# First attention of a graph network: the weights of the last 4 of 25 destination blocks on GpSimd

## The chip, the cores and the metric

The kernel runs on one core of a Trainium2 chip, as one launch. The metric is the device time of the launch in microseconds (us). The engines are named as the profile names them: PE is TensorE, DVE VectorE, ACT ScalarE, POOL GpSimd, SP SyncE (whose queue, SPq, starts DMA transfers).

## The reference

The input is x, 3125 nodes by 256 features, and 100000 edges (src, dst), sorted by dst. Two layers follow each other; each adds a graph attention and a mixer to x, and then a feed-forward part. The change lies in the graph attention of the first layer (4 heads of 64 features):

```python
h = (x @ W).reshape(N, 4, 64)
e = leaky_relu(al_s[src] + al_d[dst], 0.2)      # per edge and head
ee = exp(e - segment_max(e, dst)[dst])
alpha = ee / (segment_sum(ee, dst)[dst] + 1e-16)
out = segment_sum(h[src] * alpha[:, :, None], dst)
out = relu(out.reshape(N, 256) + bias)
```

The weight of an edge depends on the pair (src, dst) alone. So the sum over edges can be written as a sum over all pairs of nodes: the weight of the pair times the number of edges between them.

## The kernel before

Nodes are split into T = 25 blocks of R = 125. An earlier stage writes the matrix of counts (3125 by 3125, bf16) to DRAM. `stage_gat_sums` (from line 1616) does one attention; the program calls it four times, as g0a (first layer, 4 heads of 64), g1a, g2a (4 heads of 128) and g3a. With a head's width F below 128, J is 2: two heads are handled in one step. Only g0a has J = 2; the others have J = 1.

A **unit** n is one source block sb and one head: a matrix x of 125 sources by 3125 destinations. A **step** is J units with the same sb. In g0a there are NU = 100 units and NS = 50 steps: 25 steps for heads 0 and 1, then 25 for heads 2 and 3. The work on a unit goes over three engines, each with its own program, tied by semaphores:

- ACT, `rise` (line 1815): x = relu(grow * steep + minus), one instruction of 3125 columns; it counts `risen` up. It waits on `multiplied` (line 1819), since x is a ring of XR = 5 buffers.
- DVE, `weigh` (line 1748): x = (x + flat) * counts, one `scalar_tensor_tensor` at line 1755 that reads x in f32 and the counts in bf16, both in SBUF; it counts `weighed` up. The first two units are cut in three pieces of 1125, 1000 and 1000 columns.
- PE (line 1917): waits for the `weighed` of both units of the step and multiplies each destination block (in parts of 64 and 61 columns) by the features of the source block and a column of ones, into 8 PSUM banks. That is 25 x 2 x 2 = 100 products of f32, which show as 200 records each of MATMUL and LDWEIGHTS. The end of a step counts `multiplied` up, which gives two buffers back.

SP (line 1693) loads the counts of one source block per step into a ring of CR = 4 buffers and waits on `weighed` before it fills one again (line 1701). After the 25 steps of a pair of heads, ACT moves the sums out of PSUM (`move`, lines 1837 and 1840), and DVE divides them by the sum of weights (`divide`, lines 1762, 1771, 1779): eight groups of tiles for two heads, one group behind each of eight units. POOL only sets one small tile in this stage (line 1710).

The order of each engine is the order of its code: DVE's loop is at line 1796, ACT's at 1861, PE's at 1917 and, for the last two steps, 1930.

Of the kernel before, what the change touches and what calls it, by code (L numbers as in the profile page):

```python
# [5 lines left out]
ALU = mybir.AluOpType  # L6
# [7 lines left out]
N = 3125  # L14
R = 125
T = N // R
# [1599 lines left out]
def stage_gat_sums(nc, m, g, AL, HX, OUT, X=None, spare=None, ct_out=()):  # L1616

    S, G, F = g.heads, HX.shape[2], HX.shape[3] - 1
    J = 1 if F == P else 2
    NS, NU, GR, XR, CR, YR = G // J * T, G * T, G // J, 2 * J + 1, 3 if spare is None else 4, 4 if g.out == "elu" else 2  # L1620
# [4 lines left out]
    with Stage(nc, g.name + "a") as s:  # L1625
        s.sems.extend(ct_out)
        grow, x = s.sb("grow", [R, S, N]), s.sb("x", [R, XR, N])
        if spare is None:
            ct = s.sb("ct", [R, CR, N], BF16)[:]
# [16 lines left out]
        rows_in = [s.sem(f"rows_in{h}") for h in range(S)]  # L1646
        stepped, crossed, far_ready, factors = [s.sem(n) for n in ("stepped", "crossed", "far_ready", "factors")]
        spread, row_act, row_dve = [s.sem(n) for n in ("spread", "row_act", "row_dve")]
        ct_in = [s.sem(f"ct_in{k}") for k in range(CR)]
        risen, weighed, multiplied, summed, moved, divided = [s.sem(n) for n in ("risen", "weighed", "multiplied", "summed", "moved", "divided")]  # L1650
        low_ready, low_exp, y_ready = [s.sem(n) for n in ("low_ready", "low_exp", "y_ready")]
        y_out = [s.sem(f"y_out{k}") for k in range(YR)]
        block = s.block()

        def place(n):

            return n // (J * T), n // J % T, n % J

        def head(gr, j):
            return gr * J + j if S > 1 else 0  # L1660
# [18 lines left out]
        def upto(n, k=0):  # L1679

            return sum(len(sections(i)) for i in range(n)) + k + 1
# [10 lines left out]
        @block.sync  # L1692
        def _(sp):
            await_counts(sp, ct_out)
            for m_ in range(NS):
                if m_ == CR and S > 1:
                    sp.wait_ge(rows_ready, 1)
                    sp.dma_start(m.RW, turned[:]).then_inc(rows_kept, 16)
                    sp.wait_ge(rows_kept, 16)
                if m_ >= CR:  # L1700
                    sp.wait_ge(weighed, upto((m_ - CR + 1) * J) - 1)
                h, j = (m_ // T + 1) * J + (m_ % T - CR) // 5, (m_ % T - CR) % 5
                if CR <= m_ % T < CR + 5 * J and h < S:
                    sp.dma_start(grow[25 * j:25 * (j + 1), h, :], m.RW[h * T:(h + 1) * T].rearrange("t r -> (t r)").partition_broadcast(25)).then_inc(rows_in[h], 16)
                sb = m_ % T
                tile_dma(sp, ct[:, m_ % CR, :], m.CT[sb * R:(sb + 1) * R], ct_in[m_ % CR])

        @block.gpsimd
        def _(pool):
            nc.gpsimd.memset(under[:], UNDER).then_inc(stepped, 1)  # L1710
            if g.out == "elu":
                for n in range(G * CH):
                    gr, c = n // CH, n % CH
                    t0, t1 = tiles[c][0], tiles[c][-1] + 1
                    pool.wait_ge(y_ready, n + 1)
                    tile_dma(pool, OUT[t0 * R:t1 * R, gr * F:(gr + 1) * F].rearrange("(t p) f -> p t f", p=R), y[:, n % YR, 0:t1 - t0, :], y_out[n % YR])
                for k in range(YR):
                    pool.wait_ge(y_out[k], 32 * (G * CH // YR))

        @block.vector  # L1720
        def _(dve):
# [26 lines left out]
            def weigh(n):  # L1748
                gr, sb, j = place(n)
                h, step = head(gr, j), n // J  # L1750
                dve.wait_ge(ct_in[step % CR], 32 * (step // CR + 1))
                for k, (a, b) in enumerate(sections(n)):
                    dve.wait_ge(risen, upto(n, k))
                    part = x[:, n % XR, a * R:b * R]
                    nc.vector.scalar_tensor_tensor(out=part, in0=part, scalar=flat[:, h, sb:sb + 1], in1=ct[:, step % CR, a * R:b * R],  # L1755
                                                   op0=ALU.add, op1=ALU.mult).then_inc(weighed, 1)
# [118 lines left out]
        def _(pe):  # L1875
# [41 lines left out]
            for step in range(2 // J, NS - 2):  # L1917
                gr, sb = step // T, step % T
                pe.wait_ge(weighed, upto(step * J + J - 1))
                for c in range(CH):  # L1920
                    if sb == 0 and gr > 0:
                        pe.wait_ge(moved, (gr - 1) * CH + c + 1)
                    for i, piece in enumerate(pieces(c)):
                        for j in range(J):
                            done = product(step, i, j, c, *piece)
                    if c == CH - 1:
                        done.then_inc(multiplied, 1)
                    elif sb == T - 1:
                        done.then_inc(summed, 1)
            for c in range(CH):  # L1930
                for step in (NS - 2, NS - 1):
                    if c == 0:
                        pe.wait_ge(weighed, upto(step * J + J - 1))
                    for i, piece in enumerate(pieces(c)):
                        for j in range(J):
                            done = product(step, i, j, c, *piece)
                if c == CH - 1:
                    done.then_inc(multiplied, 2)
                else:
                    done.then_inc(summed, 1)  # L1940
# [1254 lines left out]
```

## Time and profile before

| | us |
|---|---|
| median of 3 runs | 3723.67 (3722.82 to 3724.9) |
| profiled execution, its own time | 3723.46 |
| its span | 3722.0 |
| mean granted clock of TensorE | 0.928 of full speed |
| first attention, first weight instruction (546.6) to the end of ACT's last move (949.4) | 402.8 |

The span runs from the first to the last instruction in the trace; the time of the execution is 1.46 us longer. "Busy" is the time in which an engine had an instruction running. "Idle before" is the time in which an engine stood still ahead of a group of instructions, with the instruction elsewhere that ended it. Durations of neighbouring instructions on DVE and ACT overlap by some tens of ns, so the distance from start to start is a little shorter than the duration. In the trace HX stands for a large tile that several stages share: in g0a both the features and the ring of counts lie in it.

### The profile page before, as it was taken

What the parts mean: (1) busy time and instruction counts of PE and PEld (TensorE: products, weight loads), DVE (VectorE), ACT (ScalarE), POOL (GpSimd) and SP (SyncE); (2) the same over time, 40 slices, a digit from 0 to 9 for tenths busy, and PEclk for the clock granted to TensorE, in tenths of its full rate; (3) what the DMA queues carried; (4) which work ended last, traced back from release to release, by engine and by line L of the source; (5) the groups of instructions that cost most, each with busy time, mean ns of one, the idle gap of its engine ahead of it and who ended that gap; (6) DMA issues with size and microseconds to landing.
All of it is one profiled execution on the core that took longest, in us unless ns stands there. A gap on an engine that the chain in (4) does not pass through costs nothing. (4 is left out here: it accounts for less than half of the span.)

```text
span 3722.0 us, 75746 instructions
## 1 busy us (share of the span) xinstructions
PE 3261.3 (88%) x32397; PEld 2992.8 (80%) x32397; DVE 2070.4 (56%) x2243; ACT 1707.3 (46%) x2005; POOL 232.3 (6%) x320
## 2 busy tenths in 40 slices
PE   3788877878469999687999999699999997999899
PEld 3568877878469998356899999679999996999676
DVE  6665558989542221653566767326767762666411
ACT  0534457878233333230555555225655552555332
POOL 1000000000012222002000100100001001000000
PEclk9879989999579999798999999899999998999889
DMA  3223345433246554301655655325656544544020
GB/s 113 51 45 51 52 85 130 119 89 88 80 169 210 185 185 144 71 12 43 160 152 155 174 140 151 85 69 159 165 143 175 146 126 129 159 136 127 6 59 27
DMA packets 176755, 424.91 MB, mean 114 GB/s; under 512 B 72469, under 2 KB 104990, under 8 KB 175052
## 3 DMA queue, kind: packets, MB, share of 16 engines
q1 hardware_dynamic: 159134, 383.68, 38.2%
q0 software_dynamic: 13904, 33.84, 3.0%
q8 instruction: 248, 4.06, 0.5%
q10 hardware_dynamic: 3399, 2.76, 0.3%
q14 instruction: 70, 0.57, 0.1%
HBM read 366.69 MB, written 53.50 MB: 113 GB/s over the span
## 5 line engine op out<-in xcount | busy, mean ns | idle before, releaser
L1904 PE MATMUL g2a_ps<-HX,g2a_x 125*125 125x129 f32 (+2 forms) x5200 | 575.2, 273 | 3.4 <-ACT g2a_grow L1858 3.3
L1904 PE MATMUL g1a_ps<-HX,g1a_x 125*125 125x129 f32 (+2 forms) x5200 | 574.9, 273 | 3.4 <-ACT g1a_grow L1858 3.4
L1904 PEld LDWEIGHTS g2a_ps<-HX,g2a_x 125*125 125x125 f32 x5200 | 574.8, 189 | 3.7 <-ACT g2a_grow L1858 3.5
L1904 PEld LDWEIGHTS g1a_ps<-HX,g1a_x 125*125 125x125 f32 x5200 | 574.6, 188 | 3.8 <-ACT g1a_grow L1858 3.6
L1755 DVE SCALAR_TENSOR_TENSOR g2a_x<-g2a_x,g2a_flat,g2a_ct 125x3125 f32<-125x3125 f32 (+2 forms) x104 | 348.2, 3350 | 183.0 <-ACT g2a_x L1812 171.4
L1755 DVE SCALAR_TENSOR_TENSOR g1a_x<-g1a_x,g1a_flat,g1a_ct 125x3125 f32<-125x3125 f32 (+2 forms) x104 | 348.2, 3350 | 182.7 <-ACT g1a_x L1812 174.3
L1812 ACT ACTIVATE g2a_x<-g2a_grow,g2a_near,g2a_steep 125x3125 f32<-125x3125 f32 (+2 forms) x104 | 300.9, 2897 | 243.1 <-PE g2a_ps L1904 242.8
L1812 ACT ACTIVATE g1a_x<-g1a_grow,g1a_near,g1a_steep 125x3125 f32<-125x3125 f32 (+2 forms) x104 | 300.9, 2897 | 242.9 <-PE g1a_ps L1904 242.6
L1904 PE MATMUL g0a_ps<-HX,g0a_x 125*64 125x65 f32 (+1 forms) x10000 | 318.1, 228 | 84.7 <-DVE g0a_x L1755 44.4
L1904 PEld LDWEIGHTS g0a_ps<-HX,g0a_x 125*64 125x64 f32 (+1 forms) x10000 | 309.8, 142 | 93.1 <-issue 45.6
L1755 DVE SCALAR_TENSOR_TENSOR g0a_x<-g0a_x,g0a_flat,HX 125x3125 f32<-125x3125 f32 (+2 forms) x104 | 341.4, 3346 | 31.4 <-ACT g0a_x L1812 31.2
L1812 ACT ACTIVATE g0a_x<-g0a_grow,g0a_near,g0a_steep 125x3125 f32<-125x3125 f32 (+2 forms) x104 | 294.9, 2892 | 83.0 <-PE g0a_ps L1904 80.3
L1904 PE MATMUL g3a_ps<-HX,g3a_x 125*125 125x129 f32 (+2 forms) x2600 | 289.2, 274 | 3.4 <-ACT g3a_grow L1858 3.4
L1904 PEld LDWEIGHTS g3a_ps<-HX,g3a_x 125*125 125x125 f32 x2600 | 288.8, 189 | 3.8 <-ACT g3a_grow L1858 3.5
L2628 ACT ACTIVATE moe_hT<-moe_psh,moe_sm 128x128 f32<-128x128 f32 x448 | 154.6, 368 | 244.6 <-PE moe_psh L2546 229.7
L1755 DVE SCALAR_TENSOR_TENSOR g3a_x<-g3a_x,g3a_flat,HX 125x3125 f32<-125x3125 f32 (+2 forms) x54 | 174.4, 3234 | 106.3 <-ACT g3a_x L1812 106.3
L2546 PE MATMUL moe_psh<-moe_xe,moe_wa 128*128 128x128 f32 x1792 | 211.8, 277 | 0.0
L1812 ACT ACTIVATE g3a_x<-g3a_grow,g3a_near,g3a_steep 125x3125 f32<-125x3125 f32 (+2 forms) x54 | 151.0, 2803 | 123.5 <-PE g3a_ps L1904 123.2
L2546 PEld LDWEIGHTS moe_psh<-moe_xe,moe_wa 128*128 128x128 f32 x1792 | 207.2, 194 | 0.1
L2608 DVE TENSOR_SCALAR moe_ys<-moe_psy,WGT 128x256 f32<-128x256 f32 x56 | 27.1, 484 | 319.8 <-PE moe_psy L2557 319.8
L706 ACT ACTIVATE HX<-merge_ps 125x500 bf16<-125x500 f32 (+1 forms) x175 | 93.9, 568 | 194.8 <-PE merge_ps L561 192.6
L2557 PE MATMUL moe_psy<-HX,moe_hT 128*128 x672 | 154.3, 379 | 0.0
(579 smaller groups left out, 3920.5 us busy)
## 6 DMA issues: line engine op xcount, KB each, us to landing
HX<-counted SPq DMA_DIRECT2D x100, 683.6 KB
g1a_ct<-counted SPq DMA_DIRECT2D x100, 683.6 KB
g2a_ct<-counted SPq DMA_DIRECT2D x100, 683.6 KB
moe_wa<-in_L_ffn_W SPq DMA_DIRECT2D x56, 1024.0 KB
counted<-HX SPq DMA_DIRECT2D x12, 1367.2 KB
HX<-counted SPq DMA_DIRECT2D x100, 79.3 KB
g1a_ct<-counted SPq DMA_DIRECT2D x100, 79.3 KB
g2a_ct<-counted SPq DMA_DIRECT2D x100, 79.3 KB
```

What stands on the lines that cost most here:

```text
L706: nc.scalar.activation(ct[:, two % 2, :, d0:d0 + n], ps[0:R, job % BANKS, 0:n * T].rearrange("p (d s) -> p s d", s=T), ACT.Copy).then_inc( ...
L1755: nc.vector.scalar_tensor_tensor(out=part, in0=part, scalar=flat[:, h, sb:sb + 1], in1=ct[:, step % CR, a * R:b * R], op0=ALU.add, op1=ALU ...
L1812: nc.scalar.activation(x[:, n % XR, a * R:b * R], grow[:, h, a * R:b * R], ACT.Relu, bias=minus[:, h, sb:sb + 1], scale=steep[:, h, sb:sb ...
L1904: return nc.tensor.matmul(ps[64 * j:64 * j + b - a, c, col:col + f1 - f0], x[:, (step * J + j) % XR, t * R + a:t * R + b], HX[:, sb, gr * ...
L2546: last = nc.tensor.matmul(psh[:, o % 4, 0:ET], wa[:, j % 3, c, o * P:(o + 1) * P], xe[:, j % XE, c, :], start=(c == 0), stop=(c == 1))
L2557: last = nc.tensor.matmul(psy[:, j % 2, 0:D], hT[:, j % 2, c, :], right, start=(c == 0), stop=(c == MH - 1))
L2608: nc.vector.tensor_scalar(ys[:, j % 2, :], psy[:, j % 2, 0:D], WGT[:, j:j + 1], None, ALU.mult).then_inc(y_ready, 1)
L2628: nc.scalar.activation(hT[:, j % 2, o, :], psh[:, o % 4, 0:ET], ACT.Gelu, bias=sm[:, j % IN, 4 + o:5 + o]).then_inc(h_ready, 1)
```

## The change

In a stage with J = 2, `share` is 21 x 125 = 2625. From unit 2 on DVE's instruction ends at column 2625. POOL gets a loop over units 2 to 99: it waits for the counts and for `risen`, adds the factor to columns 2625 to 3124 (`tensor_scalar`), drains, multiplies them by the counts (`tensor_tensor`) and counts the new semaphore `weighed_too` up. PE waits on it too before a step from step 1 on, and SP before it fills a count buffer again. Where J = 1 nothing changes.

```diff
--- before.py
+++ after.py
@@ -1646,11 +1646,13 @@
         rows_in = [s.sem(f"rows_in{h}") for h in range(S)]
         stepped, crossed, far_ready, factors = [s.sem(n) for n in ("stepped", "crossed", "far_ready", "factors")]
         spread, row_act, row_dve = [s.sem(n) for n in ("spread", "row_act", "row_dve")]
-        ct_in = [s.sem(f"ct_in{k}") for k in range(CR)]
+        ct_in, weighed_too = [s.sem(f"ct_in{k}") for k in range(CR)], s.sem("weighed_too")
         risen, weighed, multiplied, summed, moved, divided = [s.sem(n) for n in ("risen", "weighed", "multiplied", "summed", "moved", "divided")]
         low_ready, low_exp, y_ready = [s.sem(n) for n in ("low_ready", "low_exp", "y_ready")]
         y_out = [s.sem(f"y_out{k}") for k in range(YR)]
         block = s.block()
+
+        share = (T - 4) * R if J == 2 else N
 
         def place(n):
 
@@ -1699,6 +1701,8 @@
                     sp.wait_ge(rows_kept, 16)
                 if m_ >= CR:
                     sp.wait_ge(weighed, upto((m_ - CR + 1) * J) - 1)
+                    if J == 2 and m_ > CR:
+                        sp.wait_ge(weighed_too, (m_ - CR) * J)
                 h, j = (m_ // T + 1) * J + (m_ % T - CR) // 5, (m_ % T - CR) % 5
                 if CR <= m_ % T < CR + 5 * J and h < S:
                     sp.dma_start(grow[25 * j:25 * (j + 1), h, :], m.RW[h * T:(h + 1) * T].rearrange("t r -> (t r)").partition_broadcast(25)).then_inc(rows_in[h], 16)
@@ -1708,6 +1712,16 @@
         @block.gpsimd
         def _(pool):
             nc.gpsimd.memset(under[:], UNDER).then_inc(stepped, 1)
+            if J == 2:
+                for n in range(2, NU):
+                    gr, sb, j = place(n)
+                    h, step = head(gr, j), n // J
+                    pool.wait_ge(ct_in[step % CR], 32 * (step // CR + 1))
+                    pool.wait_ge(risen, upto(n))
+                    part = x[:, n % XR, share:N]
+                    nc.gpsimd.tensor_scalar(part, part, flat[:, h, sb:sb + 1], None, ALU.add)
+                    nc.gpsimd.drain()
+                    nc.gpsimd.tensor_tensor(part, part, ct[:, step % CR, share:N], ALU.mult).then_inc(weighed_too, 1)
             if g.out == "elu":
                 for n in range(G * CH):
                     gr, c = n // CH, n % CH
@@ -1751,6 +1765,8 @@
                 dve.wait_ge(ct_in[step % CR], 32 * (step // CR + 1))
                 for k, (a, b) in enumerate(sections(n)):
                     dve.wait_ge(risen, upto(n, k))
+                    if n > 1 and J == 2:
+                        b = share // R
                     part = x[:, n % XR, a * R:b * R]
                     nc.vector.scalar_tensor_tensor(out=part, in0=part, scalar=flat[:, h, sb:sb + 1], in1=ct[:, step % CR, a * R:b * R],
                                                    op0=ALU.add, op1=ALU.mult).then_inc(weighed, 1)
@@ -1917,6 +1933,8 @@
             for step in range(2 // J, NS - 2):
                 gr, sb = step // T, step % T
                 pe.wait_ge(weighed, upto(step * J + J - 1))
+                if J == 2:
+                    pe.wait_ge(weighed_too, step * J)
                 for c in range(CH):
                     if sb == 0 and gr > 0:
                         pe.wait_ge(moved, (gr - 1) * CH + c + 1)
@@ -1931,6 +1949,8 @@
                 for step in (NS - 2, NS - 1):
                     if c == 0:
                         pe.wait_ge(weighed, upto(step * J + J - 1))
+                        if J == 2:
+                            pe.wait_ge(weighed_too, step * J)
                     for i, piece in enumerate(pieces(c)):
                         for j in range(J):
                             done = product(step, i, j, c, *piece)
```

DVE's instructions at the start of g0a's loop, before (flat is the factor of each source, grow the factor row of each destination):

```order
L1794 COPY g0a_grow<-g0a_ps 125x1000 x2
L1755 SCALAR_TENSOR_TENSOR g0a_x<-g0a_x,g0a_flat,HX 125x1125
L1755 SCALAR_TENSOR_TENSOR g0a_x<-g0a_x,g0a_flat,HX 125x1000 x2
L1755 SCALAR_TENSOR_TENSOR g0a_x<-g0a_x,g0a_flat,HX 125x1125
L1755 SCALAR_TENSOR_TENSOR g0a_x<-g0a_x,g0a_flat,HX 125x1000 x2
L1755 SCALAR_TENSOR_TENSOR g0a_x<-g0a_x,g0a_flat,HX 125x3125 x51
L1762 RECIPROCAL g0a_rec<-g0a_raw 125x3
L1771 TENSOR_TENSOR g0a_raw<-g0a_raw,g0a_rec 125x3x64
L1779 SCALAR_TENSOR_TENSOR X<-g0a_raw,X 125x3x64
```

and with the change:

```order
L1810 COPY g0a_grow<-g0a_ps 125x1000 x2
L1771 SCALAR_TENSOR_TENSOR g0a_x<-g0a_x,g0a_flat,HX 125x1125
L1771 SCALAR_TENSOR_TENSOR g0a_x<-g0a_x,g0a_flat,HX 125x1000 x2
L1771 SCALAR_TENSOR_TENSOR g0a_x<-g0a_x,g0a_flat,HX 125x1125
L1771 SCALAR_TENSOR_TENSOR g0a_x<-g0a_x,g0a_flat,HX 125x1000 x2
L1771 SCALAR_TENSOR_TENSOR g0a_x<-g0a_x,g0a_flat,HX 125x2625 x51
L1778 RECIPROCAL g0a_rec<-g0a_raw 125x3
L1787 TENSOR_TENSOR g0a_raw<-g0a_raw,g0a_rec 125x3x64
L1795 SCALAR_TENSOR_TENSOR X<-g0a_raw,X 125x3x64
```

The number and the order are the same; from the third unit on the instructions have 2625 columns instead of 3125, and the divisions behind them are as they were.

POOL's instructions around the same place, before (moe_qT and moe_xin belong to the expert stage that follows):

```order
L1708 UNCONDITIONAL_BRANCH
L1710 MEMSET g0a_under 125x1
L61 UNCONDITIONAL_BRANCH
L63 ISA x7
L2503 UNCONDITIONAL_BRANCH
L2102 MEMSET moe_qT 9x1500
L2508 DMA moe_xin<-normal_rows,TOKEN 128x256 x6
```

and with the change:

```order
L1712 UNCONDITIONAL_BRANCH
L1714 MEMSET g0a_under 125x1
L1722 ISA
L1722 TENSOR_SCALAR g0a_x<-g0a_x,g0a_flat 125x500
L1724 TENSOR_TENSOR g0a_x<-g0a_x,HX 125x500
```

There are 98 such pairs of 500 columns, one for each unit from the third on, all ahead of the expert stage's first instruction on POOL.

## Rows read from the trace of the kernel before

**Rows 1.** The page: span, busy time of each engine.

```profile
span 3722.0 us, 75746 instructions
PE 3261.3 (88%) x32397; PEld 2992.8 (80%) x32397; DVE 2070.4 (56%) x2243; ACT 1707.3 (46%) x2005; POOL 232.3 (6%) x320
```

**Rows 2.** Windows: the first attention, busy us and instructions of each engine.

```profile
core 0: us, PE busy (x) PEld busy (x) DVE busy (x) ACT busy (x) POOL busy (x), PEclk, DMA share, GB/s
546.60:949.40 402.80, 318.12 (x10000) 309.76 (x10000) 362.83 (x186) 313.44 (x173) 0.00 (x0) 0.94 0.38 103
```

**Rows 3.** Groups by shape, 546 to 950 us: busy us, mean ns, idle before.

```profile
L1755 DVE SCALAR_TENSOR_TENSOR g0a_x<-g0a_x,g0a_flat,HX 125x3125 f32<-125x3125 f32 x98 | 334.2, 3471 | 31.4 <-ACT g0a_x L1812 31.2
L1755 DVE SCALAR_TENSOR_TENSOR g0a_x<-g0a_x,g0a_flat,HX 125x1000 f32<-125x1000 f32 x4 | 4.9, 1257 | 0.0
L1812 ACT ACTIVATE g0a_x<-g0a_grow,g0a_near,g0a_steep 125x3125 f32<-125x3125 f32 x98 | 287.7, 2992 | 80.5 <-PE g0a_ps L1904 80.3
```

**Rows 4.** Waits, 545 to 950 us (SPq from 530): total us, times, longest.

```profile
ACT g0a_x L1812 <- PE g0a_ps L1904: 80.3, 36, 6.0
PE g0a_ps L1904 <- DVE g0a_x L1755: 44.4, 26, 6.6
DVE g0a_x L1755 <- ACT g0a_x L1812: 31.2, 17, 7.8
DVE g0a_rec L1762 <- ACT g0a_raw L1840: 4.5, 2, 3.8
SPq L69 <- DVE g0a_x L1755: 250.6, 36, 15.8
```

**Rows 5.** Timeline (start us, us, instruction), then windows (columns as rows 2).

```profile
647.56 68.04 DVE L1755 SCALAR_TENSOR_TENSOR g0a_x<-g0a_x,g0a_flat,HX 125x3125 f32<-125x3125 f32 x20 [0.75 <-ACT g0a_x L1812]
...
754.44 3.47 DVE L1755 SCALAR_TENSOR_TENSOR g0a_x<-g0a_x,g0a_flat,HX 125x3125 f32<-125x3125 f32 x1 [7.82 <-ACT g0a_x L1812]
...
791.79 23.77 DVE L1755 SCALAR_TENSOR_TENSOR g0a_x<-g0a_x,g0a_flat,HX 125x3125 f32<-125x3125 f32 x7
...
650.53 5.89 ACT L1812 ACTIVATE g0a_x<-g0a_grow,g0a_near,g0a_steep 125x3125 f32<-125x3125 f32 x2 [0.17 <-PE g0a_ps L1904]
...
757.00:791.00 34.00, 24.55 (x626) 24.14 (x628) 31.98 (x48) 21.98 (x9) 0.00 (x0) 0.80 0.27 73
648.00:716.00 68.00, 59.96 (x1994) 58.26 (x1990) 67.50 (x20) 58.05 (x20) 0.00 (x0) 1.00 0.42 118
```

**Rows 6.** POOL's groups over the whole program: busy us, mean ns, idle before.

```profile
L1106 POOL COPY lo_xs<-XT 128x250 f32 x25 | 9.7, 397 | 209.8 <-PEq L1112 198.5 <-PE lo_ps L1123 11.3
L2102 POOL MEMSET moe_qT<- 9x1500 f32 x1 | 1.3, 1338 | 532.0 <-POOLq L64 532.0
L432 POOL MEMSET merge_qT<- 33x1000 f32 x1 | 0.9, 925 | 15.1 <-POOLq L64 15.1
L2888 POOL MEMSET ffn_e<- 128x512 f32 x1 | 0.5, 525 | 394.2 <-POOLq L64 394.2
L1710 POOL MEMSET g0a_under<- 125x1 f32 x1 | 0.1, 93 | 347.8 <-POOLq L64 347.8
```

**Rows 7.** Timeline: POOL beside DVE in the expert stage and at 1682 us.

```profile
L2508 POOL DMA_INDIRECT moe_xin<-normal_rows,TOKEN x56: 945/973/1123, 1064.6 to 1442.2; - x56
...
1180.26 1.28 DVE L2594 TENSOR_TENSOR moe_yb<-moe_yb 128x512 f32<-128x512 f32 x2
1181.27 1.12 POOL L2508 DMA_INDIRECT moe_xin<-normal_rows,TOKEN  x1 [0.30 <-issue]
...
1188.52 0.97 POOL L2508 DMA_INDIRECT moe_xin<-normal_rows,TOKEN  x1 [0.31 <-issue]
...
1681.99 0.42 DVE L2814 TENSOR_TENSOR X<-X,lo_ps 125x256 f32 x1 [18.10 <-PE lo_ps L1123]
1682.01 0.40 POOL L1106 COPY lo_xs<-XT 128x250 f32 x1 [0.42 <-PE lo_ps L1123]
```

**Rows 8.** POOL's DMA instructions of the second attention: ns min/median/max.

```profile
L69 POOL DMA_DIRECT2D attended<-g1a_y x32: 708/714/793, 1943.7 to 2366.9; - x32
L70 POOL DMA_DIRECT2D attended<-g1a_y x32: 569/577/634, 1944.5 to 2367.6; - x32
```

## The prediction

> **What bounds the kernel now.** The page's table of engines comes first: TensorE is busy for 88% of the span and POOL for 6% [rows 1], so POOL has time to give away, but an average over the whole program says nothing about one stage. The groups of instructions by line then place the edit: its new branch is taken where J is 2, and that is the first attention (g0a) alone, whose 104 weight instructions on DVE stand in [rows 3]. The stretch of that stage (first weight instruction to ACT's last move) is 402.8 us of the 3722.0, with DVE busy 362.8, TensorE 318.1, ACT 313.4 and POOL 0 [rows 2]. So this stage has another limit than the program: DVE. Its idle time is 31.2 us in front of the weights, waiting for ACT's relu, and 4.5 in front of the divisions [rows 4]. Who waits for whom confirms it: TensorE waits 44.4 us for DVE's weights, ACT 80.3 us for TensorE to give a buffer back, and the DMA queue spends 250.6 us waiting to be allowed the next count rows, so the loads are never late [rows 4].
>
> The timeline gives the beat. In the best stretches DVE runs without a gap: 20 weights in 68.04 us, 3.40 a unit, 6.80 a step of two units (2 heads) [rows 5]. ACT makes a pair of units in 5.89 and TensorE a step in 6.0 (1994 matmul records in 59.96 us, 200 to a step) [rows 5]. Around the middle each unit also carries two divisions: seven units from 754.44 to 791.79, 5.3 us each [rows 5]. The rest of the 402.8 is the start, the turn between the two passes over the blocks, and the end.
>
> **The change part by part.**
> DVE's part: 98 instructions shrink from 3125 to 2625 columns; the first two units keep their pieces. From 1000 to 3125 columns the duration goes from 1257 to 3471 ns, 1.042 ns a column [rows 3], so each saves 0.52 us and the beat falls to 2.88 us: 98 x 0.52 = **51 us of DVE time removed**.
>
> POOL's part: 98 pairs, an add with a per-partition number over 500 columns and, behind a drain, a product of 500 f32 by 500 bf16. No row of before shows either operation. The nearest row for a pass is the copy of 250 f32 columns, 397 ns; memsets of 512 and 1000 columns took 525 and 925 ns, or 0.82 ns a column [rows 6]. Low end of one pass: the memset's 0.53. High end: twice the copy, 0.79. I take the copy plus 250 more columns at 0.82, 0.60. The second pass reads two tensors: low end the same 0.53, high end two such passes one behind the other at 0.79, 1.59; I take twice 0.60, **1.2**, because the copy's row already takes more per column than the memset's, so that reading seems to cost. Pair: **1.8** (1.06 to 2.4). The Trainium skill (GPSIMD Engine Reference, Reconciling with measured numbers) gives 4497 ns for a tensor_tensor of 2048 f32 on GpSimd; an estimate from it is 1.1 us for 500 columns, and the sum below would be some 10 us less.
>
> The term that decides: can POOL's passes run beside DVE's weights? DVE's instruction reads two tensors from SBUF (x and the counts). The trace has a small case of each kind. POOL's copy beside a DVE instruction with one input in SBUF and one in PSUM: 0.40 and 0.42 us, both as when alone [rows 7]. POOL's row gather, which reads its list of rows from SBUF, takes 0.97, but 1.11 to 1.12 in 6 of 56 cases; those are the six that begin while DVE multiplies two tensors of SBUF (a pair of 512 columns, ending some 0.27 us after the gather's start) and no others [rows 7]. So what POOL wants to read seems to be kept back until DVE's two-input instruction is over. Low end: no exclusion, POOL costs nothing; high end: every pass stands between two DVE instructions and never beside one. I take the high end, since the gather is the row that is alike in what matters (two SBUF inputs on DVE). The Trainium skill (SBUF — State Buffer, Who interferes with whom) says that a VectorE instruction with two SBUF inputs and a GpSimd instruction that reads SBUF exclude each other, the later one waiting in full. By that rule the sum is the one below; with the exclusion struck out it would be the first rival's.
>
> Then the two engines are one resource. Each unit needs 2.88 + 1.8 = 4.68 us of it, a step 9.4, where ACT needs 5.9 and TensorE 6.0: both are covered. Even at the clock of 0.80 that the middle stretch shows at its 10.6 us a step TensorE is not the limit [rows 5]. Sum over the stage: -51 from DVE, +98 x 1.8 = +176 from POOL, and POOL can use about 20 of the 31.2 us in which DVE now waits for ACT: **+105 us**. The order in which they alternate changes little: whichever goes first, TensorE waits for both before it starts a step, and the ring of five buffers ties DVE to TensorE.
>
> Costs set at nothing: POOL's queue holds nothing else in this stage (one memset of 0.09 us; its next instruction, in the expert stage, comes 532.0 us after it) [rows 6]. The DMA queue's added wait stands in front of reloading a count buffer: four buffers, so it is early by about three steps, and no DVE row waits for a load [rows 4]; at risk only if a step's POOL part ran more than three steps behind, which TensorE's wait forbids. TensorE's added wait holds the whole step, though the four blocks are its last; behind it are all 100 products and, through the buffers, ACT.
>
> The profiled execution took 3723.46 us around its span of 3722.0, and the median is 3723.67: 3723.5 + 105 = 3828.5, **3829 us**.
>
> **Rivals.**
> *Side by side (faster).* The passes run beside DVE, 1.8 under 2.88. Then the beat is the ring's: ACT 2.99 + DVE 2.95 + TensorE 6.0 and a few tenths of handing over, 12.2 us for two steps, 6.1 instead of 6.80. About 34 of the 50 steps are paced by DVE now (17 waits for ACT [rows 4] mark the others): 34 x 0.7 = -24, and -8 to -34 as TensorE's clock goes. 3700. For it: the copy of [rows 7], and POOL's DMA instructions beside the same weight instructions in g1a, at a steady 714 and 577 ns, far from the 3.4 us that a wait for each would give [rows 8]; but those read no tensor from SBUF. Against it: the gather. It decides as long as POOL's pair stays under about 3.3 us.
>
> *Partial exclusion.* Only a part of each pass is kept apart (its reading, not its dispatch and writing), or the two share and both slow down: a third to two thirds of the 176 remain, 59 to 118. With the 51 taken off, and the 20 of idle time or not, that is -12 to +67; about 3755.
>
> *POOL too slow by itself.* Side by side, but the pair takes over 3.4 us. Each tenth over costs 98 x 0.1 = 10 us. My upper end, 2.4, is not enough for that, so this needs a pass twice as long as any bound here; it shares the chance of the case above, and its size.
>
> **How the numbers follow.** Full exclusion 0.63 (3756 at a pair of 1.06, from 104 - 51 - 20 = +33; 3887 at 2.4, from 235 - 51 - 20 = +164), partial exclusion or slow POOL 0.16, side by side 0.21. The predicted time is the first case's, and its own range is 3756 to 3887. The range for 8 in 10 has to take in the faster case, down to a gain of 25: 3698 to 3887. About 0.2% or 7 us is what a measurement of this kernel can tell from no change. Faster 0.20 (side by side, nearly whole), same 0.05 (the lower part of partial exclusion), slower 0.75.
>
> **What would show it.** After: DVE's weights at 2.95 us where undisturbed, and the stage at about 508 us instead of 402.8. Exclusion: weights or POOL passes that last longer than their size explains, or that begin when the other's end, never beside; TensorE waiting for POOL's product; ACT's wait for TensorE grown; the step at 9.4. Side by side: POOL's pair of 1.8 within a 2.95 us weight, the step at 6.1. The pass's size is wrong if POOL's adds and products are far from 0.60 and 1.2. I am wrong outright if the stage gets shorter, or if another stage than g0a changes by more than a few us.

## The result and the profile after

| | before | changed |
|---|---|---|
| median of 5 runs, us | 3723.67 | 3844.49 (3840.68 to 3845.61) |
| ratio, 95% interval | | 1.0333 (1.032 to 1.0347) |
| profiled span, us | 3722.0 | 3838.4 |
| first attention, first weight to ACT's last move, us | 402.8 | 520.0 |

The change costs 121 us by the medians. The predicted 3829 is 15 us below, and the time lies inside the range; that the total fits is in part luck, as shown below. In the profiled executions the span grew by 116.4 us and the first attention by 117.2, so all of it is there. The rest of the program did not move, as two windows show, after first and then before (columns as in [rows 2]):

```profile
1067.00:3838.00 2771.00, 2528.68 (x18708) 2325.99 (x18708) 1376.53 (x1557) 1177.28 (x1271) 217.91 (x299) 0.94 0.44 126
```

```profile
949.40:3722.00 2772.60, 2527.01 (x18708) 2325.47 (x18708) 1377.76 (x1560) 1178.23 (x1272) 217.49 (x299) 0.94 0.44 126
```

The changed kernel's page, its first two lines, beside [rows 1]:

```profile
span 3838.4 us, 76233 instructions
PE 3312.2 (86%) x32397; PEld 3043.2 (79%) x32397; DVE 2070.4 (54%) x2243; ACT 1706.3 (44%) x2005; POOL 705.8 (18%) x516
```

POOL went from 232.3 to 705.8 us. The window over the first attention answers to [rows 2]:

```profile
core 0: us, PE busy (x) PEld busy (x) DVE busy (x) ACT busy (x) POOL busy (x), PEclk, DMA share, GB/s
546.00:1067.00 521.00, 367.53 (x10000) 359.81 (x10000) 364.72 (x188) 313.65 (x173) 473.11 (x196) 0.83 0.29 79
```

DVE is as busy as before (364.7 us; 362.8 before), although its instructions lost 51 us of columns. ACT is unchanged. TensorE does the same 10000 records in 367.5 instead of 318.1 us, its granted clock down from 0.94 to 0.83. POOL is busy for 473 us with work that I had put at 176. The groups of the stage (busy us, mean ns, idle before):

```profile
L1722 POOL TENSOR_SCALAR g0a_x<-g0a_x,g0a_flat 125x500 f32<-125x500 f32 x98 | 280.2, 2859 | 33.7 <-ACT g0a_x L1828 33.7
L1724 POOL TENSOR_TENSOR g0a_x<-g0a_x,HX 125x500 f32<-125x500 f32 x98 | 194.9, 1988 | 14.4 <-issue 0.2
L1771 DVE SCALAR_TENSOR_TENSOR g0a_x<-g0a_x,g0a_flat,HX 125x2625 f32<-125x2625 f32 x98 | 328.4, 3387 | 144.4 <-ACT g0a_x L1828 144.1 <-issue 0.3
```

DVE's mean of 3387 ns is 0.43 us over the 2.95 that its 2625 columns take alone. POOL's means, 2.86 and 1.99 us, are together 2.24 us over the length of its two passes alone, which the next rows show.

The instructions that write the weights (ns min/median/max, first and last start):

```profile
L1771 DVE SCALAR_TENSOR_TENSOR g0a_x<-g0a_x,g0a_flat,HX x104: 1251/3366/3893, 546.0 to 1045.1; 125x2625 f32<-125x2625 f32 x98, 125x1000 f32<-125x1000 f32 x4, 125x1125 f32<-125x1125 f32 x2
L1722 POOL TENSOR_SCALAR g0a_x<-g0a_x,g0a_flat x98: 1528/2385/4813, 552.8 to 1049.0; 125x500 f32<-125x500 f32 x98
L1724 POOL TENSOR_TENSOR g0a_x<-g0a_x,HX x98: 1065/1228/3795, 557.7 to 1050.6; 125x500 f32<-125x500 f32 x98
```

The minima are the operations by themselves: 1.53 us for POOL's add, 1.07 for its product. A pass that is issued while DVE's instruction runs lasts until some time after that instruction's end. In the trace 48 of the 98 adds and 48 of the 98 products are held up like this; nearly all the others take their minimum. Seven lines of the timeline show how they stand to each other (start us, us, instruction; x2 is two instructions back to back):

```profile
703.22 5.88 ACT L1828 ACTIVATE g0a_x<-g0a_grow,g0a_near,g0a_steep 125x3125 f32<-125x3125 f32 x2 [5.85 <-PE g0a_ps L1920]
706.32 6.50 DVE L1771 SCALAR_TENSOR_TENSOR g0a_x<-g0a_x,g0a_flat,HX 125x2625 f32<-125x2625 f32 x2 [4.89 <-ACT g0a_x L1828]
706.75 4.17 POOL L1722 TENSOR_SCALAR g0a_x<-g0a_x,g0a_flat 125x500 f32<-125x500 f32 x1
711.07 2.67 POOL L1724 TENSOR_TENSOR g0a_x<-g0a_x,HX 125x500 f32<-125x500 f32 x1
713.72 1.54 POOL L1722 TENSOR_SCALAR g0a_x<-g0a_x,g0a_flat 125x500 f32<-125x500 f32 x1
713.88 2.42 PE L1920 MATMUL g0a_ps<-HX,g0a_x 125*64 125x65 f32 x42 [2.87 <-POOL g0a_x L1724]
...
721.49 5.88 ACT L1828 ACTIVATE g0a_x<-g0a_grow,g0a_near,g0a_steep 125x3125 f32<-125x3125 f32 x2 [4.55 <-PE g0a_ps L1920]
```

ACT hands over the first unit at 706.2. DVE starts on it at 706.32, and POOL's add is issued at 706.75, but it ends only at 710.92, 1.39 us behind the end of DVE's first instruction at 709.53. (That one took 3.21 us and met the end of an earlier product of POOL's; the second took 3.37.) DVE has the second unit under way by then. POOL's product, issued at 711.07, has to wait for that one too and ends at 713.74, 0.92 behind it. TensorE starts at 713.88. This first unit is the one that completes TensorE's step. From ACT's handing over to TensorE's start it takes **7.7 us**, where DVE's one instruction of 3.47 stood before. Who waits for whom, beside [rows 4]:

```profile
ACT g0a_x L1828 <- PE g0a_ps L1920: 195.9, 46, 9.2
DVE g0a_x L1771 <- ACT g0a_x L1828: 144.1, 41, 8.0
PE g0a_ps L1920 <- POOL g0a_x L1724: 120.9, 44, 7.8
PE g0a_ps L1920 <- DVE g0a_x L1771: 18.6, 5, 6.6
```

TensorE now waits 120.9 us for POOL; it waited 44.4 for DVE. ACT waits 195.9 us (80.3) for buffers from TensorE, DVE 144.1 us (31.2) for ACT. Three of the four engines wait for each other. POOL does not: from its first pass at 552.8 to the end of its last at 1051.7 us it waits 11.4 us for ACT (33.7 less the 22.3 before its first pass) and loses 14.4 in the gaps between add and product. It has become the engine that the stage goes by, at 499 us for 98 units or **5.1 us a unit**: 2.6 us of passes, 2.2 of being held up behind DVE, and the gaps.

### The profile page after: what moved, and what is told of

Its sections match the earlier page's. It is cut to its first block and busy times, and to the rows that moved or that the text cites. A ratio compares the mean times of both kernels' runs of the same rounds, so it can differ in the third digit from the quotient of the medians.

```text
span 3838.4 us, 76233 instructions
## 1 busy us (share of the span) xinstructions
PE 3312.2 (86%) x32397; PEld 3043.2 (79%) x32397; DVE 2070.4 (54%) x2243; ACT 1706.3 (44%) x2005; POOL 705.8 (18%) x516
## 5 line engine op out<-in xcount | busy, mean ns | idle before, releaser
L1920 PE MATMUL g0a_ps<-HX,g0a_x 125*61 125x65 f32 (+1 forms) x10000 | 367.5, 245 | 152.2 <-POOL g0a_x L1724 120.9
L1920 PEld LDWEIGHTS g0a_ps<-HX,g0a_x 125*61 125x61 f32 (+1 forms) x10000 | 359.8, 159 | 160.0 <-issue 147.2
L1771 DVE SCALAR_TENSOR_TENSOR g2a_x<-g2a_x,g2a_flat,g2a_ct 125x3125 f32<-125x3125 f32 (+2 forms) x104 | 348.2, 3350 | 183.2 <-ACT g2a_x L1828 180.1
L1771 DVE SCALAR_TENSOR_TENSOR g0a_x<-g0a_x,g0a_flat,HX 125x2625 f32<-125x2625 f32 (+2 forms) x104 | 335.7, 3266 | 144.4 <-ACT g0a_x L1828 144.1
L1828 ACT ACTIVATE g0a_x<-g0a_grow,g0a_near,g0a_steep 125x3125 f32<-125x3125 f32 (+2 forms) x104 | 295.2, 2887 | 198.4 <-PE g0a_ps L1920 195.9
L1722 POOL TENSOR_SCALAR g0a_x<-g0a_x,g0a_flat 125x500 f32<-125x500 f32 x98 | 280.2, 2859 | 33.7 <-ACT g0a_x L1828 33.7
L1724 POOL TENSOR_TENSOR g0a_x<-g0a_x,HX 125x500 f32<-125x500 f32 x98 | 194.9, 1988 | 14.4 <-issue 0.2
```

The lines of the kernel that those rows point to most:

```text
L1722: nc.gpsimd.tensor_scalar(part, part, flat[:, h, sb:sb + 1], None, ALU.add)
L1724: nc.gpsimd.tensor_tensor(part, part, ct[:, step % CR, share:N], ALU.mult).then_inc(weighed_too, 1)
L1828: nc.scalar.activation(x[:, n % XR, a * R:b * R], grow[:, h, a * R:b * R], ACT.Relu, bias=minus[:, h, sb:sb + 1], scale=steep[:, h, sb:sb ...
L1920: return nc.tensor.matmul(ps[64 * j:64 * j + b - a, c, col:col + f1 - f0], x[:, (step * J + j) % XR, t * R + a:t * R + b], HX[:, sb, gr * ...
```

## Experiments

In what follows "products end" is the last product's start in the profiled execution, and the stage is measured as in the table above. Ratios are to the kernel before, timed on the same chip beside each run: 3720.04 us beside e1 to e4, 3715.82 beside e5 to e8. The stage in a profiled execution varies by more than that: unchanged it took 402.8 us before and 395.7 in e8, on another chip. So a gain of a few us is read from the medians. The cuts are against the changed kernel and show only the lines that matter. In e1, e2, e3, e4 and e6 ACT's bias is changed as e1's cut shows.

### e1: nobody makes the last four blocks' weights

POOL's whole loop goes, and SP's wait on it.

```diff
-                    nc.gpsimd.tensor_scalar(part, part, flat[:, h, sb:sb + 1], None, ALU.add)
-                    nc.gpsimd.drain()
-                    nc.gpsimd.tensor_tensor(part, part, ct[:, step % CR, share:N], ALU.mult).then_inc(weighed_too, 1)
...
-                    pe.wait_ge(weighed_too, step * J)
...
-                nc.scalar.activation(x[:, n % XR, a * R:b * R], grow[:, h, a * R:b * R], ACT.Relu, bias=minus[:, h, sb:sb + 1],
+                nc.scalar.activation(x[:, n % XR, a * R:b * R], grow[:, h, a * R:b * R], ACT.Relu, bias=(flat if J == 2 and n > 1 else minus)[:, h, sb:sb + 1],
```

> Left out: the weights of the last four blocks are not made by any engine (ACT's bias is the positive factor, so that no sum is zero), and nobody waits for GpSimd. It shows what VectorE's shorter instruction is worth alone. Every theory expects the same here: VectorE 2.95 us an instruction, the first attention 375 to 385 us instead of 402.8, the kernel about 25 us under before, 3700. If it is not under before at all, the 51 us taken off VectorE were never on the path, and the whole +121 is GpSimd's.

Measured: 3710.76, ratio 0.9974 (0.9962 to 0.9986), a gain of about 10 us where some 25 were expected; the stage takes 392.8 us, not 375 to 385. So the 51 us taken from DVE are worth about 10, not the 24 of my faster rival. The window that held 20 units before [rows 5]:

```profile
648.00:716.00 68.00, 57.83 (x1842) 56.60 (x1839) 55.12 (x20) 53.27 (x20) 0.00 (x0) 0.95 0.41 111
```

DVE is busy for 55 of 68 us instead of 67.5, and the beat is no faster. (The x20 counts each instruction that touches the window; TensorE's records make 9.2 steps of 200, where they made 10.0 before, at a clock of 0.95 instead of 1.00.) The gain lies later: 39 units from 788.46 to 920.23 us, or 6.76 a step, where the kernel before made 35 from 791.79 to 917.37, or 7.18. The 6.1 us of my faster rival shows in one stretch only, eight units in 24.4 us:

```profile
826.07 11.66 DVE L1759 SCALAR_TENSOR_TENSOR g0a_x<-g0a_x,g0a_flat,HX 125x2625 f32<-125x2625 f32 x4 [0.77 <-ACT g0a_x L1816]
838.32 11.72 DVE L1759 SCALAR_TENSOR_TENSOR g0a_x<-g0a_x,g0a_flat,HX 125x2625 f32<-125x2625 f32 x4 [0.58 <-ACT g0a_x L1816]
850.45 5.84 DVE L1759 SCALAR_TENSOR_TENSOR g0a_x<-g0a_x,g0a_flat,HX 125x2625 f32<-125x2625 f32 x2 [0.41 <-ACT g0a_x L1816]
```

The waits say what took over (the stretch is 545 to 950 us):

```profile
ACT g0a_x L1816 <- PE g0a_ps L1908: 72.4, 36, 6.3
DVE g0a_x L1759 <- ACT g0a_x L1816: 69.4, 34, 9.7
PE g0a_ps L1908 <- issue: 41.9, 27, 3.9
PE g0a_ps L1908 <- DVE g0a_x L1759: 28.4, 16, 6.6
```

TensorE stands still for 41.9 us with nothing that the profile can name, 27 times, for up to 3.9 us; ACT waits for TensorE, and DVE for ACT. The kernel before had these pauses too (its waits, then two lines of its timeline):

```profile
PE g0a_ps L1904 <- issue: 37.0, 23, 3.7
...
655.91 7.68 PE L1904 MATMUL g0a_ps<-HX,g0a_x 125*61 125x65 f32 x256 [0.70 <-issue]
664.19 6.44 PE L1904 MATMUL g0a_ps<-HX,g0a_x 125*61 125x65 f32 x209 [0.60 <-issue]
```

Here 256 products lie between two pauses. Counted through the stage, all 23 pauses of the kernel before stand a whole multiple of 128 MATMUL records apart, and so do the 27 of e1. So they belong to places in TensorE's sequence of instructions and not to DVE's data. With them TensorE cannot keep up 6.0 us a step, and relieving DVE brings little. What they are was not tested.

### e2: GpSimd's passes on data of its own, nobody waits

The waits on POOL are left out as in e1; `apart` has 460 columns and `m.all` is the table of constants.

```diff
-                    part = x[:, n % XR, share:N]
-                    nc.gpsimd.tensor_scalar(part, part, flat[:, h, sb:sb + 1], None, ALU.add)
+                    part = apart[:]
+                    nc.gpsimd.tensor_scalar(part, m.all[0:R, 0:460], flat[:, h, sb:sb + 1], None, ALU.add)
...
-                    nc.gpsimd.tensor_tensor(part, part, ct[:, step % CR, share:N], ALU.mult).then_inc(weighed_too, 1)
+                    nc.gpsimd.tensor_tensor(part, part, m.all[0:R, 500:960], ALU.mult).then_inc(weighed_too, 1)
```

> As the run without GpSimd, but GpSimd makes its 98 pairs of passes on data of its own (460 columns, read from the constants), behind the same signal of ACT, and nobody waits for it. Exclusion (both want the same way to SBUF): VectorE's instructions last 3.5 to 3.9 us wherever a pass stands beside them, its pitch is 2.88 plus one pass's reading, about 3.6 us, and the products end 30 to 60 us later than without GpSimd; GpSimd gets one pass per VectorE instruction, lags to half and runs on alone for some 100 us behind it. Rival (the waits on GpSimd's slow chain are the cost, not the port): VectorE stays at 2.95 us, the products end where they do without GpSimd, and GpSimd's passes stay at 1.54 and 1.07 us.

Measured: 3821.68, ratio 1.0275 (1.0257 to 1.0292), but where the time lies matters. The products end at 947.9, 11.5 us later than in e1 (936.4) and where they did before (947.8); counted from each run's first weight it is 10 us. The timeline:

```profile
698.12 14.16 DVE L1773 SCALAR_TENSOR_TENSOR g0a_x<-g0a_x,g0a_flat,HX 125x2625 f32<-125x2625 f32 x4
699.64 2.84 POOL L1725 TENSOR_TENSOR g0a_apart<-g0a_apart,C 125x460 f32<-125x460 f32 x1
702.73 3.81 POOL L1723 TENSOR_SCALAR g0a_apart<-C,g0a_flat 125x460 f32<-125x460 f32 x1 [0.25 <-issue]
706.68 2.84 POOL L1725 TENSOR_TENSOR g0a_apart<-g0a_apart,C 125x460 f32<-125x460 f32 x1
709.77 3.80 POOL L1723 TENSOR_SCALAR g0a_apart<-C,g0a_flat 125x460 f32<-125x460 f32 x1 [0.25 <-issue]
```

No data tie the two engines together here, and yet each slows the other. DVE's pitch is 3.54 us (14.16 by 4) instead of 2.88. POOL gets one pass per DVE instruction in this stretch: a pair every 7.04 us, two DVE pitches. So it falls behind and runs on alone after the products, with passes that now last 1.43 and 1.15:

```profile
1050.05 1.43 POOL L1723 TENSOR_SCALAR g0a_apart<-C,g0a_flat 125x460 f32<-125x460 f32 x1 [0.25 <-issue]
1051.63 1.15 POOL L1725 TENSOR_TENSOR g0a_apart<-g0a_apart,C 125x460 f32<-125x460 f32 x1
```

The stage's closing barrier waits for that queue, 105 us past the products; that is the 102 us of this run, not a slower ring. The exclusion is shown. My 30 to 60 us for the products was too much: what DVE lost (0.66 a unit in this stretch, 0.53 in the mean) is about what it had gained by its fewer columns.

### e3: all waits, but passes that only write

```diff
-                    nc.gpsimd.tensor_scalar(part, part, flat[:, h, sb:sb + 1], None, ALU.add)
...
-                    nc.gpsimd.tensor_tensor(part, part, ct[:, step % CR, share:N], ALU.mult).then_inc(weighed_too, 1)
+                    for _k in range(4):
+                        nc.gpsimd.memset(apart[:], 1.0)
+                        nc.gpsimd.drain()
+                    nc.gpsimd.memset(apart[:], 1.0).then_inc(weighed_too, 1)
```

> All waits of the change are kept, but GpSimd's pair is replaced by five memsets of 460 columns, together some 2.6 us, the length of an undisturbed pair; they write SBUF and read nothing. Left out: the weights of the last four blocks (ACT's bias is the positive factor). Exclusion of readers: within 10 us of the run without GpSimd, 3700 to 3715, and VectorE at 2.95 us. Rival (the chain of waits is the cost): most of the +116 stays, 3800 or more.

Measured: 3714.6, ratio 0.9987 (0.9977 to 0.9998), 4 us above e1. DVE is undisturbed:

```profile
L1774 DVE SCALAR_TENSOR_TENSOR g0a_x<-g0a_x,g0a_flat,HX x104: 1252/2954/2958, 544.7 to 917.1; 125x2625 f32<-125x2625 f32 x98, 125x1000 f32<-125x1000 f32 x4, 125x1125 f32<-125x1125 f32 x2
```

A chain of 2.9 us on POOL (from the first memset's start to the fifth's end; the real pair, undisturbed in e4, takes 2.8) with every wait of the change costs next to nothing as long as it reads nothing from SBUF. The waits alone are not the cause.

### e4: GpSimd's real passes beside a DVE instruction with one input

```diff
+                    if n > 1 and J == 2:
+                        nc.vector.tensor_reduce(least_of[:, n:n + 1], part, AX_X, ALU.max).then_inc(weighed, 1)
+                        continue
                     nc.vector.scalar_tensor_tensor(out=part, in0=part, scalar=flat[:, h, sb:sb + 1], in1=ct[:, step % CR, a * R:b * R],
                                                    op0=ALU.add, op1=ALU.mult).then_inc(weighed, 1)
```

> The changed kernel with its GpSimd passes and all its waits, but VectorE's instruction on units from the third on is a maximum over the same 2625 columns into a number of its own: one input from SBUF instead of two, about the same length. Left out: the weights of the 21 blocks. If two inputs are what excludes GpSimd: passes at 1.54 and 1.07 us always, the first attention 375 to 390 us, 3695 to 3715. Rival (any VectorE instruction that reads SBUF excludes GpSimd): passes of 2.7 and 4.2 us as in the changed kernel and 3830 or more.

Measured: 3719.36, ratio 0.9997 (0.9984 to 1.0009).

```profile
L1724 POOL TENSOR_SCALAR g0a_x<-g0a_x,g0a_flat x98: 1527/1535/2032, 551.9 to 926.6; 125x500 f32<-125x500 f32 x98
L1774 DVE TENSOR_REDUCE g0a_least_of<-g0a_x x98: 2874/2887/2890, 552.4 to 926.5; 125x1 f32<-125x2625 f32 x98
L1726 POOL TENSOR_TENSOR g0a_x<-g0a_x,HX x98: 1062/1132/1292, 554.1 to 928.3; 125x500 f32<-125x500 f32 x98
```

POOL reads and writes the same data as in the change, and its passes stay at 1.54 and 1.13 us, DVE's at 2.89. Only three adds (1.72 to 2.03 us) and one product (1.29) are longer, and each of the four meets an instruction of DVE that still has two inputs. So it is not DVE's reading as such that keeps POOL out. The maximum differs from the weights in a second thing: it writes one column and not 2625. That DVE's writing does no harm is shown by a smaller case, the copy of [rows 7]: 0.40 us, as when alone, beside a DVE instruction that writes 256 columns and reads one input from SBUF and one from PSUM. With it the second input from SBUF is what remains, though no run took that input away and left the rest of the instruction as it was. The time is 9 us above e1 and 4 over my upper bound; even with no exclusion the change would have given nothing that can be measured.

### e5 and e6: one pass each

e5, the add alone:

```diff
-                    nc.gpsimd.tensor_scalar(part, part, flat[:, h, sb:sb + 1], None, ALU.add)
-                    nc.gpsimd.drain()
-                    nc.gpsimd.tensor_tensor(part, part, ct[:, step % CR, share:N], ALU.mult).then_inc(weighed_too, 1)
+                    nc.gpsimd.tensor_scalar(part, part, flat[:, h, sb:sb + 1], None, ALU.add).then_inc(weighed_too, 1)
```

e6, the product alone:

```diff
-                    nc.gpsimd.tensor_scalar(part, part, flat[:, h, sb:sb + 1], None, ALU.add)
-                    nc.gpsimd.drain()
```

> The change with GpSimd's first pass alone (the add); left out: the product with the counts in the last four blocks. All waits stay. Theory A (two engines share one resource: the cost is the sum of busy time, as the prediction summed it): a pass of 1.54 us by 98 is 151, less 51 and 20: +80, about 3800. Theory B (only a pass's reading excludes VectorE, some 0.67 us of the add, and GpSimd gets one pass per VectorE instruction; what costs is TensorE's wait for GpSimd's last pass of a step): of the pair's chain behind the second VectorE instruction (product 0.9, add 1.6, product 1.07) the add alone stays, so +20 to +60, 3745 to 3780; passes of 4.2 us and of 1.54 in equal numbers.

> The change with GpSimd's second pass alone (the product); left out: the add in the last four blocks (ACT's bias is the positive factor). Theory A (sum of busy time): 1.07 by 98 is 105, less 51 and 20: +34, 3755. Theory B (one pass per VectorE instruction, TensorE waits for the last one): behind the second VectorE instruction of a step only one product of 0.9 to 1.07 us stays, so +0 to +45, 3720 to 3765, and less than the add alone.

Measured: the add alone 3733.27, ratio 1.0047 (1.0031 to 1.0064), +17 us; the product alone 3735.51, ratio 1.0053 (1.0036 to 1.0069), +20 us. First e5, then e6:

```profile
L1769 DVE SCALAR_TENSOR_TENSOR g0a_x<-g0a_x,g0a_flat,HX x104: 1253/3350/3369, 547.6 to 945.0; 125x2625 f32<-125x2625 f32 x98, 125x1000 f32<-125x1000 f32 x4, 125x1125 f32<-125x1125 f32 x2
L1722 POOL TENSOR_SCALAR g0a_x<-g0a_x,g0a_flat x98: 1538/3310/4817, 554.3 to 945.9; 125x500 f32<-125x500 f32 x98
```

```profile
L1769 DVE SCALAR_TENSOR_TENSOR g0a_x<-g0a_x,g0a_flat,HX x104: 1251/3757/3941, 546.1 to 944.4; 125x2625 f32<-125x2625 f32 x98, 125x1000 f32<-125x1000 f32 x4, 125x1125 f32<-125x1125 f32 x2
L1722 POOL TENSOR_TENSOR g0a_x<-g0a_x,HX x98: 1067/2740/3799, 552.8 to 942.6; 125x500 f32<-125x500 f32 x98
```

The sum of busy time gave +80 and +34; e5 refutes it clearly, e6 by 14 us. The add alone is also a little under the +20 to +60 of the other theory, and its passes were not half long and half short: 92 of 98 are held up. A pass keeps DVE out only for part of its length: DVE's median is 3350 ns beside adds (+0.40) and 3757 beside products (+0.80). In e6 DVE hardly waits for ACT (15.0 us in all), so its longer instructions are the cost: 0.26 us over the 3.47 of before, times 98, is 25. That the product would cost less than the add was wrong: they are equal. The stage takes 416.0 and 416.8 us, 20 and 21 above the unchanged one of e8. And 17 and 20 do not add up to 121, nor do 27 and 30, their distance from e1's gain, to 131: two passes a unit cost much more than twice one.

### e7: one block instead of four

```diff
-        share = (T - 4) * R if J == 2 else N
+        share = (T - 1) * R if J == 2 else N
```

> The change with one block of 125 columns for GpSimd instead of four. Theory A (sum of busy time) with passes a quarter as long plus a fixed part, about 0.5 and 0.4 us: 98 x 0.9 = 88, less 98 x 0.13 = 13 and 20: +55, 3775. Theory B (the alternation, not the columns, is what costs): VectorE's instruction is hardly shorter (3.34 us) and GpSimd still waits for one of them ahead of each pass, so passes last 3.8 to 4 us where they wait; the chain behind the second VectorE instruction shrinks from 3.9 to some 1.5 us: +30 to +75. The two are told apart less by the time than by the passes: under B they last over 3 us though they have 125 columns.

Measured: 3794.71, ratio 1.0218 (1.0201 to 1.0235), +79 by the medians: a quarter of the columns, two thirds of the cost. (DVE is also relieved of less here, 13 us instead of 51, but e1 puts the worth of all 51 at 10.) The stage takes 475.2 us, 79.5 over the unchanged one of e8.

```profile
701.28 3.64 POOL L1722 TENSOR_SCALAR g0a_x<-g0a_x,g0a_flat 125x125 f32<-125x125 f32 x1
...
705.06 3.00 POOL L1724 TENSOR_TENSOR g0a_x<-g0a_x,HX 125x125 f32<-125x125 f32 x1
708.04 0.61 POOL L1722 TENSOR_SCALAR g0a_x<-g0a_x,g0a_flat 125x125 f32<-125x125 f32 x1
708.80 0.40 POOL L1724 TENSOR_TENSOR g0a_x<-g0a_x,HX 125x125 f32<-125x125 f32 x1
```

Passes of 125 columns last 0.61 and 0.40 us alone and 3.64 and 3.00 where they wait for DVE. What costs is that two passes a unit are held up behind DVE instructions, far more than what they do. POOL is no longer busy throughout: it waits 60 us for ACT once it has begun (82.0 less 22.3), so here it is the delay of the unit that TensorE waits for that counts. The cost is a little over the upper end that I gave.

### e8: the same split in the last attention instead

```diff
-        share = (T - 4) * R if J == 2 else N
+        shared = g.out == "plain"
+        share = (T - 4) * R if shared else N
```

> The same split of the weights, undone in the first attention and put into the last one (g3a: one head per step of 5.72 us, VectorE idle for 106 us, TensorE the limit; 48 pairs of passes). The exclusion is there too: adds of about 4.2 us that wait for the VectorE instruction of the same unit. But the add and the product then fit behind it: 2.95 + 1.6 + 1.07 = 5.6 under 5.72, and the ring of three buffers gives 11.4 us. Expected: within 5 us of before, 3715 to 3728. Rival (GpSimd's passes cost wherever they are put): 48 of 98 pairs, so about half of +121, 3780.

Measured: 3722.29 against 3715.82, ratio 1.0022 (1.0012 to 1.0032). Two units of g3a:

```profile
3294.18 2.95 DVE L1772 SCALAR_TENSOR_TENSOR g3a_x<-g3a_x,g3a_flat,HX 125x2625 f32<-125x2625 f32 x1 [2.77 <-ACT g3a_x L1829]
3294.25 4.29 POOL L1723 TENSOR_SCALAR g3a_x<-g3a_x,g3a_flat 125x500 f32<-125x500 f32 x1 [0.22 <-ACT g3a_x L1829]
...
3298.68 1.07 POOL L1725 TENSOR_TENSOR g3a_x<-g3a_x,HX 125x500 f32<-125x500 f32 x1
...
3299.90 2.95 DVE L1772 SCALAR_TENSOR_TENSOR g3a_x<-g3a_x,g3a_flat,HX 125x2625 f32<-125x2625 f32 x1 [2.77 <-ACT g3a_x L1829]
```

The exclusion is the same: each add waits for the DVE instruction of its unit and takes 4.29 us. But DVE has one unit per 5.72 us there, so the product comes at once and undisturbed, 5.57 us behind DVE's start (3294.18 to 3299.75), before the next instruction of DVE. TensorE waited for POOL only this long:

```profile
PE g3a_ps L1921 <- POOL g3a_x L1725: 4.0, 2, 2.3
```

TensorE is the limit in this attention, so that a delay has slack to go into as well. Its products take from 3167.1 to 3459.2 us, 292.1, where they took 289.0 before (3173.7 to 3462.7). The median is 6.5 us above; some 3 of them are seen in that stage, where the rest lies is open.

## Why the prediction was right, and what was wrong in it

**What bounds the kernel: half right.** DVE did set the beat at 6.80, but the next limit was put at 6.1 us a step, from TensorE's 6.0. The row with TensorE's unnamed pauses (37.0 us) was left out of the argument. With them e1 comes to 6.76 us a step in its better half, against 7.18 before, and gains 10 us, not 24. The faster rival was worth 0.3%, close to nothing.

**DVE's part, -51 us: right in size.** 2950 ns an instruction were forecast and 2953 measured in e1. It was not worth that much on the path. Nor did POOL use 20 us of DVE's idle time: DVE's wait for ACT grew from 31.2 to 144.1 us.

**POOL's part: mis-sized, one up, one down.** The add was put at 0.60 (bounds 0.53 to 0.79) and takes 1.54; the product at 1.2 and takes 1.07. The copy at 397 ns for 250 columns was the wrong neighbour of an add with a number per partition. e7 gives the add two points, 0.61 us at 125 columns and 1.54 at 500: 2.5 ns a column against the 0.82 that I took from the memsets. The pair is 2.6 us, over the 2.4 of my high end. The estimate of 1.1 us for the product, worked out from the figure of the Trainium skill (GPSIMD Engine Reference, Reconciling with measured numbers), agrees with the 1.07 measured.

**The deciding term, exclusion: right, and shown.** The gather's 0.15 us [rows 7] pointed the right way. e2 shows it with no data tie, e3 removes POOL's reading and e4 DVE's second input (and most of its writing), and it vanishes both times. The rule of the Trainium skill (SBUF — State Buffer, Who interferes with whom) names just this pair, and says that a GpSimd instruction that only writes goes free, and so does a VectorE instruction with one input from SBUF, outside its two-port modes; e3 and e4 agree. It also calls the shared ports an exclusive lock, held for the whole instruction. For POOL behind DVE that holds (passes of 4.17 and 2.67). For DVE behind POOL the runs show less: 0.40 us for an add that lasts 1.54.

**"The two engines are one resource", 4.68 us a unit, +105: the step that failed.** It gave nearly the right total by the wrong sum, and by luck. With the pair as measured, 2.6 us, the same sum gives 256 - 51 - 20 = +185. The pair that was too short made up for an exclusion that was taken too hard: I let every pass stand between two DVE instructions, on DVE's account, and what DVE loses to POOL in the changed kernel is 0.43 us a unit, 43 us in all. By DVE's account the stage would have become shorter, 43 - 51 - 20 = -28; even with the 0.40 and 0.80 of e5 and e6 for every unit it would have grown by 98 x 1.2 - 51 - 20 = +47 and not by 117.

What the runs showed in its place is that POOL pays. It is held up for 2.2 us a unit and needs 5.1, and nearly without idle time it sets the pace of the stage. "The order in which they alternate changes little" was the false sentence. For the unit that completes a step POOL's two passes stand behind two DVE instructions, its own and the next one's. That makes 7.7 us out of 3.5 in the ring that ties ACT, DVE, POOL and TensorE. Once round in the timeline's numbers: ACT's pair starts at 703.22 in a buffer just given back, TensorE starts on its first unit's step at 713.88, and with the end of that step ACT starts again at 721.49. That is 18.3 us for two steps, where DVE's beat made 13.6; it is one of the shortest rounds of the stage, and most take 19 to 22, since POOL is often still busy with the unit before. e5 and e6 (one pass: +17 and +20), e7 (small passes: +79) and e8 (a DVE instruction that has no next one close behind, and slack beside TensorE: about nothing) fit this and not the sum. How the 117 us divide between POOL's full queue and the delay of the step's last unit was not separated. Nor was a kernel tried in which TensorE waits for POOL only ahead of the last four blocks, as their weights alone come from POOL.

**TensorE's clock: seen, not foreseen.** I held TensorE to be covered at any clock. It is in the ring, with 49.4 us more busy time for the same products at 0.83, and its step in the round above takes 7.6 us instead of 6.0. In this stage it stands still for 153 us, where it did for 85 before. In e7 it is busy for 347.4 us at 0.88; in e5 and e6, which cost little, for 319.0 and 318.6 at 0.95 and 0.94. So part of the cost of the two dear kernels may be the clock. How much lies on the path was not separated; that POOL waits only 11.4 us for ACT speaks for little of it in the changed kernel.

**The added waits at nothing: right by themselves** (e3), and wrong together with the exclusion. SP's was right: it now waits 397.0 us for POOL before it fills a count buffer, but no engine waits for a load.

## What to carry to other kernels

In these runs work moved from VectorE to GpSimd ran beside it only where VectorE's instruction had one input in SBUF, or GpSimd's read none; check that before counting columns. Where they exclude each other, count GpSimd's passes, each of which can cost up to a whole VectorE instruction of waiting, and see whether GpSimd still keeps up and whether somebody waits for its last pass. And before an engine is relieved, ask what the next limit is, pauses without a name included: here the whole relief of 51 us would have bought 10.

## What the runs showed of the hardware

- POOL's add of a number per partition to 500 f32 columns takes 1.54 us, longer than the two-tensor product of the same size (1.07).
- A POOL pass of 500 columns issued while DVE works on two SBUF tensors ends 1.4 us (add) or 0.93 us (product) behind DVE's end (median of 48 each in the changed kernel). A DVE instruction that meets a pass is 0.40 us (add, e5) or 0.80 us (product, e6) longer by the median.
- With both queues full neither starved the other in e2: they took turns, one pass to one instruction, at 3.54 us a turn.
- POOL's memsets beside the same DVE instruction (483 ns for 460 columns) and its passes beside a DVE maximum over one tensor (medians of 1.54 and 1.13 us) are not touched.
- TensorE's unnamed pauses in the stage, 23 of them and 37.0 us in the kernel before, all stand a whole multiple of 128 MATMUL records apart.
